# A state-space and mixture-of-experts layer: exp/ln reordered with a second drain buffer, skip term spread, inputs of the scan moved in wide blocks

## The reference, cut to what matters

```
x   = in_proj_w @ ctx                 # 512 -> 1024 channels
u   = silu(conv4(x) + conv_b)
dt_lo, Bm, Cm = split(x_proj_w @ u, [32, 16, 16])
delta = softplus(dt_proj_w @ dt_lo + dt_proj_b)
state[n,t] = exp(delta[t]*A[n]) * state[n,t-1] + delta[t]*u[t]*Bm[n,t]
y[t] = sum_n state[n,t]*Cm[n,t] + D*u[t]
y    = y * silu(layernorm(x_residual))
```

## Time and profile before

| what | value |
|---|---|
| median of 3 runs | 4564.35 us (4563.07 to 4567.16) |
| the profiled execution | 4560.37 us, span of its trace 4558.4 us |
| mamba_inputs | 0 to 622 us of the span |
| selective_scan | 622 to 1967 us |
| the rest | 1967 to 4558 us |
| busy share, whole span | TensorE 87%, VectorE 67%, ScalarE 48%, GpSimd 40% |

### The profile page before, as it was taken

One profiled execution on the slowest core, in us unless ns is written; L12 is line 12 of the kernel. 1 busy time (PEld: TensorE's weight loads), 2 busy tenths in 40 slices (PEclk: granted clock), 3 DMA queues, 4 the chain that ended last, 5 costly groups with the idle time before them and its releaser, 6 DMA issues. The chain is left out here.

```text
span 4558.4 us, 59565 instructions
## 1 busy us (share of the span) xinstructions
PE 3953.5 (87%) x21344; PEld 3174.1 (70%) x21344; DVE 3031.4 (67%) x3537; ACT 2183.1 (48%) x2185; POOL 1833.7 (40%) x1020
## 2 busy tenths in 40 slices
PE   8787338878878878859999979999999999899999
PEld 3333227767767767748888857777777777688887
DVE  6666449979979979967787744554555554355555
ACT  2666538878878878822222233444444444311111
POOL 0343439989989989933323310000000000022221
PEclk9988659999999999979999989999999999999999
DMA  6677564464454454443333346666666666466433
GB/s 229 209 235 229 164 188 112 112 169 108 110 168 110 112 162 110 107 159 126 134 124 134 115 153 222 222 215 210 211 219 209 209 211 211 180 230 227 155 123 106
DMA packets 500326, 767.93 MB, mean 168 GB/s; under 512 B 76288, under 2 KB 306432, under 8 KB 500160
## 3 DMA queue, kind: packets, MB, share of 16 engines
q1 hardware_dynamic: 468128, 698.42, 47.4%
q0 software_dynamic: 31744, 67.23, 5.0%
q10 hardware_dynamic: 288, 0.07, 0.0%
HBM read 596.30 MB, written 202.81 MB: 175 GB/s over the span
## 5 line engine op out<-in xcount | busy, mean ns | idle before, releaser
L863 POOL TENSOR_TENSOR h<-h,c 128x1024 f32<-128x1024 f32 x512 | 1208.6, 2408 | 121.6 <-DVE h L846 121.6
L846 DVE TENSOR_TENSOR_SCAN h<-da,dbu 128x1024 f32<-128x1024 f32 x512 | 1134.3, 2272 | 157.1 <-ACT dbu L812 96.6
L880 PE MATMUL psb<-m,du_taps 128*128 128x128 f32 x4096 | 579.0, 289 | 240.7 <-ACT dbu L812 149.8
L880 PEld LDWEIGHTS psb<-m,du_taps 128*128 128x128 f32 x4096 | 507.0, 195 | 347.4 <-ACT dbu L812 189.1
L1717 DVE TENSOR_TENSOR wsp<-raw,wsp 128x4096 fp32r<-128x4096 f32 x96 | 424.7, 4425 | 336.0 <-ACT wsp L1674 336.0
L819 ACT ACTIVATE da<-dl,ad 128x1024 f32<-128x1024 f32 x512 | 584.8, 1142 | 72.2 <-DVE h L846 57.1
L812 ACT ACTIVATE dbu<-psb 128x1024 f32<-128x1024 f32 x512 | 522.2, 1020 | 164.4 <-PE psb L880 157.7
L890 PE MATMUL psy<-ident,h 128*128 128x128 f32 x4096 | 550.2, 278 | 10.3 <-POOL h L863 6.1
L1583 POOL DMA_INDIRECT xg<-scratch_xn,ids x64 | 63.4, 990 | 1140.7 <-PE psT L1603 1124.3
L890 PEld LDWEIGHTS psy<-ident,h 128*128 128x128 f32 x4096 | 443.2, 142 | 18.5 <-DVE aux L838 8.7
L1674 ACT ACTIVATE wsp<-raw 128x4096 fp32r<-128x4096 f32 x96 | 347.3, 3619 | 9.8 <-DMA raw<-in_w 9.6
(11 more groups left out here) (189 smaller groups left out, 7811.7 us busy)
## 6 DMA issues: line engine op xcount, KB each, us to landing
raw<-in_w SPq DMA_DIRECT2D x96, 2048.0 KB
du_taps<-scratch_duT SPq DMA_DIRECT2D x512, 128.0 KB, 3.3
scratch_duT<-duT SPq DMA_DIRECT2D x64, 512.0 KB, 4.0
c<-scratch_c SPq DMA_DIRECT2D x64, 512.0 KB, 7.3
scratch_ob<-ob SPq DMA_DIRECT2D x64, 512.0 KB, 11.0
xs<-in_x SPq DMA_DIRECT2D x32, 512.0 KB, 5.5
scratch_u<-u SPq DMA_DIRECT2D x32, 512.0 KB, 5.5
xz<-in_x SPq DMA_DIRECT2D x32, 512.0 KB, 4.0
```

The lines of the kernel that those rows point to most:

```text
L846: dve.tensor_tensor_scan(h[:, k % HR, :], da[k % 2][:, :], dbu[:, (k // GN) % 2, k % GN, :], 0.0, ALU.mult, ALU.add).then_inc(s_scan, 1)
L863: pool.tensor_tensor(h[:, k % HR, :], h[:, k % HR, :], c[:, n, :], ALU.mult).then_inc(s_hc, 1)
L880: mm = pe.matmul(psb[:, j], duT[:, r * CP + j, :], m[:, :, r * CP + j, g * GN:(g + 1) * GN], start=True, stop=True)
```

## The change

Part one, in `mamba_inputs`:

- `softplus` keeps Relu and Abs. The Exp pair becomes `exp_pair`, after an explicit load of the table set that holds both exp and ln, in the same (odd) step. The Ln pair becomes `log_pair`, one step later, right after `du_head`.
- The late odd tiles' `dt_proj` writes the bank of `psD` (now `psW`) in place of `psV`, and `dt_proj(q)` of a late tile waits for `abs` of tile q-2, not q-1. The late `relu` moves on VectorE from behind `convolve` to before `correction`.

Part two, in both parts:

- The transposes of du and Bm take every 8th time step (`t::ET`), so that a partition of `duT` holds 8 neighbouring steps: du is stored and loaded in runs of 4 KB. A scan time is now t*32+c in place of c*32+t, so that ScalarE's eviction reads `psb` at a stride of 512 bytes and writes runs of 8 elements.
- Bm is stored (runs of 256 bytes, each row twice) on the diagonals of bands that are zero elsewhere. The scratch `bT` grows to 4*2*2*32*4352 floats, 8.91 MB; `clear_b` zeroes it in one transfer of 8704 runs of 1 KB, issued by SyncE in step 3.
- `m` is split into two halves of 8 states. Each half is loaded by 8 transfers of 16 rows of 8 KB, as soon as its own last reader is done.
- The skip term is added at sets 6 to 9, a quarter at each.

```diff
-        bT = sb("bT", [P, 2, ET, NST], F32R)
+        bT = sb("bT", [P, 2, 2, ET, NH], F32R)
+        zero = sb("zero1", [P, ROW])
+        def dt_bank(q):
+            return psW if late(q) and q % 2 else psV
             def store_b(b):
-                        sp.dma_start(dr["bT"][b, c].rearrange("t (j k) n -> k t j n", k=P // TB)[k],
-                                     f32(bT[k * TB:(k + 1) * TB, c % 2])).then_inc(s_btst, 16)
+                            diagonal = bass.AP(band.tensor, band.offset + twin * BAND * ROW + k * ET * NH,
+                                               [[SKEW, TB], [TB * SKEW, 2], [1, ET * NH]])
+                            sp.dma_start(diagonal, f32(bT[k::P // TB, part]).rearrange("t h j n -> t h (j n)"))\
+                                .then_inc(s_btst, 16)
             def store_du(q):
-                    sp.dma_start(dr["duT"][q, part].rearrange("(t p) e -> p t e", p=P), f32(duT[:, part]))\
+                    sp.dma_start(dr["duT"][q, part].rearrange("t (k j) e -> (t k) j e", j=ET), f32(duT[:, part]))\
+            def clear_b():
+                sp.wait_ge(s_zero, 1)
+                bands = dr["bT"].rearrange("b c h z -> (b c h z)").rearrange("(p r z) -> p r z", p=P, z=ROW)
+                sp.dma_start(bands, zero[:].unsqueeze(1).to_broadcast([P, bands.shape[1], ROW])).then_inc(s_btz, 16)
             def step(s):
                 on_tile(s, 0, load_stats)
+                if s == 3:
+                    clear_b()
                 on_tile(s, DUT, store_du)
...
             def dt_proj(q):
-                after(pe, s_abs, q)
-                after(pe, s_relu, q - (Q - ET))
+                after(pe, s_abs, q - 1 if late(q) and q > Q - ET else q)
             def du_transpose(q):
-                    mm = pe.transpose(du_bank(q)[:, t, :], ebuf[:, q % SR, t * P:(t + 1) * P], ident[:])
+                    mm = pe.transpose(du_bank(q)[:, t, :], ebuf[:, q % SR, t::ET], ident[:])
...
+            def exp_pair(q):
                 if q % 2:
+                    act.preload_act_table_set("natural_log_exp_and_others")
                     act.wait_ge(s_abs, q + 1)
...
             def step(s):          # ScalarE
                 on_tile(s, DUT, du_head)
+                on_tile(s, DT + 1, log_pair)
                 on_tile(s, USILU, u_silu)
...
                 on_tile(s, DT, softplus)
+                on_tile(s, DT, exp_pair)
                 on_tile(s, SZT, gate_copy)
...
             def step(s):          # VectorE
+                on_tile(s, DT, lambda q: relu(q) if late(q) else None)
                 on_tile(s, LOG, correction)
                 on_tile(s, LOG + 1, lambda q: times_u(dve, q) if tail(q) else None)
                 on_tile(s, 0, convolve)
-                on_tile(s, DT, lambda q: relu(q) if late(q) else None)
...
-        GATED, SKIPPED = 1, 8
+        GATED, SKIPPED = 1, 6
-        m = sb("m", [P, TB, NC, NST], F32R)
+        m = sb("m", [P, 2, TB, NC, NH], F32R)
...
-            def load_m(b):
+            def load_m(b, half):
                 if b:
-                    sp.wait_ge(s_mm, b * ET * NST)
+                    sp.wait_ge(s_mm, (b * ET - 1) * NST + (half + 1) * NH)
-                for t in range(TB):
-                    sp.dma_start(f32(m[t::TB, t]), dr["bT"][b, :, t]).then_inc(s_m, 16)
+                for part in range(2):
+                    for a in range(TB // BAND):
+                        band = dr["bT"][b, part, half]
+                        rows = bass.AP(band.tensor, band.offset + a * BAND * SKEW, [[BAND * ROW, 2 * BAND], [1, BAND * ROW]])
+                        p0 = part * 2 * TB + a * 2 * BAND
+                        sp.dma_start(f32(m[p0:p0 + 2 * BAND, half, a * BAND:(a + 1) * BAND]).rearrange("p t c n -> p (t c n)"),
+                                     rows).then_inc(s_m[half], 16)
...
-            load_m(0)
+            load_m(0, 0)
+            load_c(0, 0)
+            load_m(0, 1)
...
+                if turned:
+                    load_m(b, 1)
...
+                if turn:
+                    load_m(b, 0)
                 for r in range(PARTS):
-                    if turn and r == PARTS - 1:
-                        load_m(b)
...
-                act.activation(dbu[:, g % 2, :, r * CP * TB:(r + 1) * CP * TB],
-                               psb[:].rearrange("p c t n -> p n (c t)"), ACT.Copy).then_inc(s_ev, 1)
+                act.activation(dbu[:, g % 2].rearrange("p n (t c) -> p n t c", c=NC)[:, :, :, r * CP:(r + 1) * CP],
+                               psb[:].rearrange("p c t n -> p n t c"), ACT.Copy).then_inc(s_ev, 1)
```

More of the change, by code:

```diff
@@ L29 @@
 GN = 4
+NH = NST // 2
+BAND = 8
+ROW = NC * NH
+SKEW = 2 * BAND * ROW + ROW
 ALU = mybir.AluOpType
@@ L299, in store_b @@
                 sp.wait_ge(s_btlo, b + 1)
-                for c in range(4):
-                    for k in range(P // TB):
-                        sp.dma_start(dr["bT"][b, c].rearrange("t (j k) n -> k t j n", k=P // TB)[k],
-                                     f32(bT[k * TB:(k + 1) * TB, c % 2])).then_inc(s_btst, 16)
+                if b == 0:
+                    sp.wait_ge(s_btz, 16)
+                for part in range(2):
+                    for twin in range(2):
+                        for k in range(P // TB):
+                            band = dr["bT"][b, part]
+                            diagonal = bass.AP(band.tensor, band.offset + twin * BAND * ROW + k * ET * NH,
+                                               [[SKEW, TB], [TB * SKEW, 2], [1, ET * NH]])
+                            sp.dma_start(diagonal, f32(bT[k::P // TB, part]).rearrange("t h j n -> t h (j n)"))\
+                                .then_inc(s_btst, 16)
             def store_delta(q):
@@ L418, in b_transpose @@
                 for t in range(ET):
-                    mm = pe.transpose(vT[:, t, 0:NST], xd[DR:DR + NST, t * P:(t + 1) * P], ident[DR:DR + NST, DR:DR + NST])
+                    mm = pe.transpose(vT[:, t, 0:NST], xd[DR:DR + NST, t::ET], ident[DR:DR + NST, DR:DR + NST])
                 mm.then_inc(s_bttr, 1)
@@ L536, in _ @@
         def _(dve):
+            dve.memset(zero[:], 0.0).then_inc(s_zero, 1)
             cv = Steps(dve, s_cv, DC - 1)
@@ L692, in selective_scan @@
         s_zero = sem("p2_matrix_zero")
-        s_m = sem("p2_matrix_loaded")
+        s_m = [sem(f"p2_matrix_loaded{half}") for half in range(2)]
         s_du = [sem(f"p2_du_loaded{r}") for r in range(PARTS)]
@@ L875, in multiply_b @@
                     pe.wait_ge(s_du[r], i * 64 + 64)
-                if k % (ET * NST) == 0:
-                    pe.wait_ge(s_m, (i // ET + 1) * TB * 16)
+                if k % (ET * NST) in (0, NH):
+                    pe.wait_ge(s_m[k % (ET * NST) // NH], (i // ET + 1) * 2 * TB // BAND * 16)
                 after(pe, s_ev, k)
                 for j in range(CP):
-                    mm = pe.matmul(psb[:, j], duT[:, r * CP + j, :], m[:, :, r * CP + j, g * GN:(g + 1) * GN], start=True, stop=True)
+                    mm = pe.matmul(psb[:, j], duT[:, r * CP + j, :], m[:, g // 2, :, r * CP + j, g % 2 * GN:(g % 2 + 1) * GN], start=True, stop=True)
                 mm.then_inc(s_mm, 1)
@@ L896, in add_state @@
                     pe.wait_ge(s_ut, i * 16 + 16)
-                    for t in range(ET):
+                if 0 <= n - SKIPPED < ET // 2:
+                    for t in (2 * (n - SKIPPED), 2 * (n - SKIPPED) + 1):
                         mm = pe.matmul(psy[:, t, :], ut[:, t * P:(t + 1) * P], skip[:], start=False, stop=False)
-                    mm.then_inc(s_skip, 1)
+                    if n == SKIPPED + ET // 2 - 1:
+                        mm.then_inc(s_skip, 1)
             for k in range(SETS + BEHIND):
```

50 lines of the change are left out of this document (30 added, 20 removed).

## The result

The kernel after takes 4466.29 us (median of 4 runs, 4463.64 to 4468.80), the kernel before beside it 4565.76 us: a ratio of 0.978, 95% interval 0.977 to 0.980. Predicted were 4446 us, 4405 to 4500. The profiled execution took 4464.75 us, its span is 4463.0 us. The first table compares the parts with the terms of the prediction; a part begins with GpSimd's first instruction in it.

A forecast was written before the change was run, and what follows sets the result against it. It took TensorE's nearly gapless steps, then a ring of short waits, to bound mamba_inputs, and GpSimd selective_scan. Terms of -26 - 8 - 20.5 + 18 - 9.5 - 54 - 18 = -118 gave 4446 us, range 4405 to 4500.

The forecast's parts named there:

- rival with strided weights: TensorE's du transposes in mamba_inputs: weight reads at 32 bytes cost 20 us, giving 4466 us; chance 0.17.
- Exp and Ln, steady: Steady steps of mamba_inputs: gap before du_transpose shrinks, 2.6 us gained a pair over 10 pairs, -26 us (-15 to -40).
- Store of Bm: SyncE's queue in mamba_inputs: issues at 0.5 us each, two stalls lose 4 us each, -8 us (0 to -12).
- End of mamba_inputs: Last steps of mamba_inputs: late steps 8.7 us each, plus gains in steps behind them, -20.5 us (-10 to -26).
- clear_b: SyncE's queue, early mamba_inputs: the clear takes 33 us, blocks later loads and delays in_proj(6), +18 us (+8 to +32).
- Start of the scan: Start of selective_scan: eight transfers in place of 32 before the first multiply, -9.5 us (-6 to -12).
- Batch turns: Three batch turns in selective_scan: m's halves load earlier, GpSimd's wait shrinks, 18 us each, -54 us (-35 to -60).
- the turns keep a wait: Rival at the scan's batch turns: half 1 of m is late by 6 to 8 us, giving 4470 us; chance 0.10.
- Skip term: Units of selective_scan: adding it in quarters shrinks both bubbles, 0.55 of 0.77 us in 32 units, -18 us (0 to -24).
- Strides: Scan eviction's strided reads and the transposes' strided weights: no change taken, 20 us kept for the range.
- slower rival: Scan's eviction becomes the bound: gain gone at +0.3 us each, 4930 us at twice the time; chance 0.07.
- Table load: ScalarE in mamba_inputs: one load (1.28 us) less per pair; rival that it stays, 4459 us, chance 0.04.

The follow-up runs named there:

- e5: Kernel after with du transposes reading 128 neighbouring columns, not every 8th (it computes another scan, same amount of work): 4465.0 us, ratio 0.978.
- e1: Kernel before with part one alone (Exp and Ln pairs, second drain buffer, relu moved); scan and weights as before: 4529.3 us, ratio 0.993.
- e2: Kernel after without part one; wide blocks, clear, strided weights and spread skip term stay: 4500.7 us, ratio 0.987.
- e10: Kernel after without the second drain buffer: dt_proj writes psV for every tile and waits for the tile before: 4467.0 us, ratio 0.979.
- e12: Kernel after with the clear in 9 pieces a batch and the stores of Bm issued four in each of four steps: 4436.2 us, ratio 0.972.
- e11: Kernel after with each batch's 16 stores of Bm issued four in each of four steps: 4448.0 us, ratio 0.975.
- e3: Kernel after with the clear cut into 9 pieces for each batch, one in each step's place in the queue: 4456.6 us, ratio 0.976.
- e4: Kernel after with the skip term added in one go, in front of its unit's gate: 4482.9 us, ratio 0.983.

## Why the prediction was right, and where not

The direction, the range and the two changed parts' shares held; the time was 20 us above the point: four terms were too hopeful, by 12, 4, 2 and 9 us, and the clear cost some 6 us less than in the sum. That the misses partly cancel is luck. The rival with strided weights also gives 4466 us. That is a coincidence: e5 shows 1 to 2 us there. By its steps:

- **Exp and Ln, steady (-26): mis-sized, -14 in e1 from the first du transpose on, and -1.6 before it.** An ordinary odd step gained what was said (14.8 to 11.55), and that "TensorE's 1.7 us from the higher clock are used up" in the even step held (12.75 before, 12.69 after). The step that failed is the price of VectorE's scales, "0.4 us a pair on average". Where they meet `b_rest`, in steps 19 and 27, the whole gain is gone (0.2 and 0.1 us in e1): the prediction saw VectorE as the limit of step 31 only and counted these two among its 10. Where they do not, in steps 15 and 23, `dt_proj` waits in the next even step, 1.1 and 1.3 us in e1, 0.9 and 3.0 in the kernel after, where the second wait also took the clock. That is 2.2 us in place of 0.8 for each set of scales in e1. The rest is step 21, with a store of Bm in the queue (1.3 us short) and the even steps 18 and 26, 1.6 and 2.8 us longer in e1; no run explains these two.
- **Store of Bm (-8): mis-sized, -4 in e2.** "At the 0.5 us of other transfers" failed: an issue took 0.71 us with a quarter of the runs, as before.
- **End of mamba_inputs (-20.5): right in sum (-20.2), partly by luck.** The late steps are 8.53 us apart, 8.7 predicted. The 5 us given to the second bank are not the bank's (e10): that step goes from 18.22 to 11.94 us with one bank as with two. So they come from the rest of part one, the order of Ln and relu and the table load; no run separates these. The step behind the last relu gave 6.6 us, not 4, and the step with the queue's hold-up lost 2.7 us, not 1.5. The hold-up by the queue came as said: VectorE's `du_rest` waited 5.65 us, until 532.7, for the store of duT.
- **clear_b (+18): mechanism right, size off.** The queue behind it was blocked for 22.8 us, near the lower bound of 23 and far from the 33 chosen: the extrapolation from short runs of other transfers failed. At `in_proj(6)` it cost 13.7 us. "Nothing of it comes back" nearly held: some 2 us do, 13.7 at `in_proj(6)` are 11 to 12 at the end of the part (e12 against e11, and e3 against after with e3's 3 us of clock).
- **Start of the scan (-9.5): -7.6,** within its bounds.
- **Batch turns (-54): -45 by GpSimd's idle time.** Half 1 was not what was late. The wait was for du, with half 0 just ahead of it, which the prediction did not name: it counted only SyncE's order, not that `c`, `m` and du together fill the DMA engines for 30 us. 5 us stay at each turn, not 2. The 9 us that are missing lie between the sum and the rival "the turns keep a wait" (18 to 24), with another transfer at fault.
- **Skip term (-18): right.** -15 by e4's scan, -20 by GpSimd's idle time outside the start and the turns (21.7 us before, 1.2 after). The bubbles are almost all gone, more than the 0.55 of 0.77 us a unit that was expected.
- **Strides (0): right** within 1 to 2 us; the eviction is at 1.022 us against 1.020. The slower rival, an eviction as the bound, is out.
- **Table load:** gone, 16 fewer.

## What to carry to other kernels

When a gap on the bounding engine closes, ask which other engine has the least slack over the whole pattern, not in the average step: its periodic extra work (here the scales) comes back as a wait, and sometimes twice, when the clock falls behind it. Before counting a gain for every step, look at the steps with extra work one by one: a closed gap is worth only what the next wait leaves. A queue that issues in order is a resource of its own: 16 small issues or one huge transfer in one place delay whatever stands behind, so spread them instead of moving them; moving only chooses another victim. Look at what stands behind the moved transfer before reordering.

## What the runs showed of the hardware

- A transfer of 8.91 MB was issued in 0.65 us, but SyncE could issue only one more in the following 22.8 us, and that one waited; cut into 36 pieces of up to 256 KB (e3) the same bytes blocked nothing: no issue next to a piece took over 1.5 us.
- The issue of `store_b`'s small transfers cost the same with runs of 64 bytes (11.77 us for 16) and of 256 bytes (11.43 us), while the DMA engines were 24% and 13% busy.
- At the turn the full DMA engines moved 388 GB/s in one stretch, with rows of `c` under way, and 188 GB/s in the next, with `m` (16 partitions, 8 KB runs) and du (128 KB each) under way: a full busy share says nothing of the rate.
- Weights read at a stride of 32 bytes took 18.7 us against 17.0 us for 144 loads (197 against 151 ns each); ScalarE's read of PSUM at 512 bytes took 1022 ns, at 16 bytes 1020.
- A short wait of TensorE did not always cost its clock: 8 matmuls took 5.29 us (mean granted clock 0.68, so in part at 1.2 GHz) behind a wait of 2.68 us in the kernel after, and 3.59 us (clock 1.00) behind one of 2.78 us in e1.
